# Loads and the large store of a graph layer moved from SyncE's queue to GpSimd's

## What is computed

```python
keep = (u >= 0.1).astype(x.dtype)
x_drop = x * keep / (1.0 - 0.1)
r = x + jnp.matmul(adj, x_drop)          # adj 8192 x 8192, x and u 8192 x 64, all fp32
m = jnp.mean(r, axis=-1, keepdims=True)
v = jnp.var(r, axis=-1, keepdims=True)
return (r - m) / jnp.sqrt(v + 1e-05)
```

## Time and profile before

| | us |
|---|---|
| median of 3 runs | 641.73 (641.69 to 641.83) |
| the profiled execution | 641.88 |
| its span | 640.1 |
| mean granted TensorE clock | 0.922 of full speed |
| PE busy | 502.8 (79% of the span) |
| DVE, ACT, POOL busy | 53.7, 17.7, 1.6 |
| HBM read, written | 272.63 MB, 2.10 MB: 429 GB/s over the span |

### The profile page before, as it was taken

One profiled execution on the slowest core, in us unless ns is written; L12 is line 12 of the kernel. 1 busy time (PEld: TensorE's weight loads), 2 busy tenths in 40 slices (PEclk: granted clock), 3 DMA queues, 4 the chain that ended last, 5 costly groups with the idle time before them and its releaser, 6 DMA issues.

```text
span 640.1 us, 5097 instructions
## 1 busy us (share of the span) xinstructions
PE 502.8 (79%) x2312; PEld 179.7 (28%) x2312; DVE 53.7 (8%) x102; ACT 17.7 (3%) x41; POOL 1.6 (0%) x14
## 2 busy tenths in 40 slices
PE   0097969688799578879878689867869868689997
PEld 0062213232233222223222223222323223133344
DVE  1930001010010100101000010100101001010101
ACT  0001000000000000000000000000000000000000
POOL 1000000000000000000000000000000000000000
PEclk9997979988799978889979899978999969799999
DMA  9999999999999999999999999999999999999998
GB/s 393 459 394 455 431 420 454 405 446 439 422 421 436 435 451 422 438 408 444 459 418 434 442 412 455 420 434 446 426 418 426 446 451 422 438 405 438 425 425 364
DMA packets 7207, 274.84 MB, mean 429 GB/s; under 512 B 800, under 2 KB 928, under 8 KB 1312
## 3 DMA queue, kind: packets, MB, share of 16 engines
q1 hardware_dynamic: 7056, 272.63, 98.8%
q10 hardware_dynamic: 144, 2.10, 0.8%
HBM read 272.63 MB, written 2.10 MB: 429 GB/s over the span
## 4 chain that ended last, share of the span: by engine, by line
DMA 62%; PE 33%; DVE 3%; another core or an unknown queue 1%; issue 0%; ACT 0%; SPq 0%; DVEq 0%; ACTq 0%
DMA ring<-adj 56%; PE acc L202 33%; DMA ring<-adj_last 5%; DMA xdrop<-u 2%; DVE node_sum L317 1%; DVE xdrop L321 1%; DVE xdrop L329 1%; PE folded L210 0%; DVE x_sb L321 0%; PE lifted L237 0%; SPq L126 0%; ACT squares L303 0%; PE lifted L263 0%; ACT std L308 0%
## 5 line engine op out<-in xcount | busy, mean ns | idle before, releaser
L202 PE MATMUL acc<-ring,xdrop 128*64 128x512 f32 (+1 forms) x2176 | 485.6, 606 | 103.1 <-DMA ring<-adj 101.7
L202 PEld LDWEIGHTS acc<-ring,xdrop 128*64 128x64 f32 x2176 | 162.8, 146 | 413.0 <-issue 280.2
L344 DVE SCALAR_TENSOR_TENSOR y<-folded,x_sb 128x256 f32<-128x256 f32 (+1 forms) x16 | 6.7, 416 | 552.3 <-PE folded L210 552.3
L237 PE MATMUL lifted<-x_sb,lift 128*128 128x64 f32 x4 | 1.1, 428 | 30.6 <-DVE x_sb L321 30.6
L210 PEld LDWEIGHTS folded<-fold,sums_T 128*128 128x128 f32 x128 | 15.5, 191 | 12.6 <-issue 12.6
L284 ACT COPY sums_T<-acc 128x512 f32<-128x512 f32 x15 | 8.8, 585 | 335.0 <-PE acc L202 335.0
L210 PE MATMUL folded<-fold,sums_T 128*128 128x64 f32 x128 | 17.7, 281 | 0.0
L277 ACT ACTIVATE std<-square_sum,eps 128x4 f32<-128x4 f32 (+1 forms) x16 | 4.8, 297 | 225.2 <-DVE square_sum L351 225.2
L237 PEld LDWEIGHTS lifted<-x_sb,lift 128*128 128x128 f32 x4 | 0.9, 322 | 30.5 <-issue 30.5
L348 DVE TENSOR_TENSOR squares<-y 128x256 f32<-128x256 f32 (+1 forms) x16 | 6.7, 417 | 0.5
L355 DVE TENSOR_TENSOR x_sb<-y,rstd 128x256 f32 (+1 forms) x16 | 6.7, 416 | 0.6
(11 more groups left out here) (23 smaller groups left out, 5.5 us busy)
## 6 DMA issues: line engine op xcount, KB each, us to landing
ring<-adj SPq DMA_DIRECT2D x13, 4096.0 KB, 31.3
ring<-adj SPq DMA_DIRECT2D x2, 2048.0 KB, 28.7
xdrop<-u ACTq DMA_DIRECT2D x1, 2048.0 KB, 12.5
x_sb<-x SPq DMA_DIRECT2D x1, 2048.0 KB, 12.3
out<-x_sb SPq DMA_DIRECT2D x1, 1984.0 KB, 12.7
ring<-adj_last SPq DMA_DIRECT2D x1, 1920.0 KB, 29.5
ring<-adj_last SPq DMA_DIRECT2D x1, 1792.0 KB, 33.4
ring<-adj_last SPq DMA_DIRECT2D x1, 1536.0 KB, 30.6
```

What stands on the lines that cost most here:

```text
L202: last = nc.tensor.matmul(acc[i][D * h:D * h + D, 0:cols], xdrop[:, k, :], piece[:, b, :], start=(k < 2), stop=(k >= NB - 2))
L344: nc.vector.scalar_tensor_tensor(out=y[:, 0:nj, :], in0=folded[:, 0:nj, :], scalar=1.0 / KEEP, in1=x_sb[:, bass.ds(block0, nj), :], op0=AL ...
```

## The change

The block of GpSimd now issues row 0, row 1, then makes its constants, and then issues all other loads of the matrix and the large store, with the same waits on `half_used` and `rows_ready`. SP keeps x, the last store and the final waits. The loop over t is gone: GpSimd's program is written out for rows 2 to 30. With no loop, rows 10 and 20 can be loaded as row 30 is, in one half and two quarters that signal `late_in`, and `late_free` with its memsets is gone. The large store has a semaphore of its own, `bulk_stored`. On PE the two products `lifted<-x_sb,lift` and their waits move from ahead of row 0 to behind it.

```diff
         @block.sync
         def _(sp):
             sp.dma_start(x_sb[:, :, :], x[:, :, :]).then_inc(x_in, 16)
-
+            sp.wait_ge(rows_ready, FINAL + 1)
+            sp.dma_start(out[:, NB - LAST_J:NB, :], x_sb[:, NB - LAST_J:NB, :]).then_inc(stored, 16)
+            sp.wait_ge(stored, 16)
+            sp.wait_ge(bulk_stored, 16)
+
+        @block.gpsimd
+        def _(pool):
             def load(r, w, first, count, arrived):
 
                 b = ((2 * w + 1) * HALF + first * QUARTER) % (RING * HALF)
-                sp.dma_start(ring[:, b:b + count * QUARTER, :],
+                pool.dma_start(ring[:, b:b + count * QUARTER, :],
                              adj[r - 1, :, first * QUARTER:(first + count) * QUARTER, :]).then_inc(arrived, 16)
...
-                sp.wait_ge(half_used, r * 2 + (half - (RING - 1)))
+                pool.wait_ge(half_used, r * 2 + (half - (RING - 1)))
...
-            sp.dma_start(narrow[:, first_narrow:first_narrow + LAST_PB, :],
+            pool.dma_start(narrow[:, first_narrow:first_narrow + LAST_PB, :],
                          adj_last[0, :, :, :]).then_inc(row_in[0], 16)
             whole(1, 1)
-            for w in range(2, WRAP):
-                free(w, 1)
-                whole(w, w)
-            wrapped(WRAP)
-            with sp.Fori(1, ROWS // RING - 1) as t:
...
-            for n in range(2):
-                nc.gpsimd.memset(late_free[:, n:n + 1], 0.0).then_inc(late_in[n], (ROWS // (2 * RING) - 1) * 16)
             nc.gpsimd.memset(eps[:, :], EPS).then_inc(eps_ready, 1)
...
+            for r in range(2, ROWS):
+                if r % RING == WRAP:
+                    wrapped(r)
+                    continue
+                free(r, 1)
+                if r % (2 * RING):
+                    whole(r, r % RING)
+                else:
+
+                    load(r, 0, 0, 2, row_in[0])
+                    for n in range(2):
+                        load(r, 0, 2 + n, 1, late_in[n])
+            for n, (k, size) in enumerate(parts):
+
+                free(ROWS, (k + size - 1) // (2 * HALF))
+                pool.dma_start(narrow[:, last_narrow + k:last_narrow + k + size, :],
+                             adj_last[1, :, k:k + size, :]).then_inc(part_in[n], 16)
+
+            pool.wait_ge(rows_ready, FINAL)
+            pool.dma_start(out[:, 0:NB - LAST_J, :], x_sb[:, 0:NB - LAST_J, :]).then_inc(bulk_stored, 16)
...
-            pe.wait_ge(lift_ready, 1)
-            pe.wait_ge(x_centred, 1)
-            for j in range(LAST_J):
-                nc.tensor.matmul(lifted[:, j, 0:D], lift[:, :], x_sb[:, NB - LAST_J + j, :], start=True, stop=False)
             pe.wait_ge(fold_ready, 1)
...
+            pe.wait_ge(lift_ready, 1)
+            pe.wait_ge(x_centred, 1)
+            for j in range(LAST_J):
+                nc.tensor.matmul(lifted[:, j, 0:D], lift[:, :], x_sb[:, NB - LAST_J + j, :], start=True, stop=False)
```

More of the change, by code:

```diff
@@ L60, in graph_layernorm @@
         node_sum = sb("node_sum", [P, 2, NB])
-        late_free = sb("late_free", [P, 2])
         fold = sb("fold", [P, D])
@@ L114, in graph_layernorm @@
         rows_ready = sem("rows_ready")
+        bulk_stored = sem("bulk_stored")
         stored = sem("stored")
```

## The result

The changed kernel takes 643.82 us (median of 7 runs, 643.76 to 644.12) against 641.83 us for the kernel before beside it (641.69 to 642.0): ratio 1.0032, 95% interval 1.0021 to 1.0043, 2.0 us slower. The forecast was 642.3, in a range of 637 to 652. The profiled execution took 643.76 us with a span of 642.0, against 640.1.

A forecast was written before the change was run, and what follows sets the result against it. The prediction took the DMA engines, 99.7% busy, as the bound. Span 640.1 + 0.1 (code) + 0.4 (pieces) + 0.1 (end) = 640.7, then + 1.78 outside the span - 0.15 to the median = 642.3 us, range 637 to 652.

The forecast's parts named there:

- The bound: Whole kernel: DMA queues fill 99.7% of the span, PE is busy 79%, so time is bytes over rate.
- equal rate: Loads in mid-kernel: GpSimd's queue moves bytes at the rate of SP's, 430 GB/s from 59 to 639 us.
- Rivals 2: Load transfers: a lower rate from more, smaller descriptors or lagging engines, 1 to 2.4%, 648 to 656 us; chance 0.17.
- rival 4: Long stretch of loads: GpSimd's queue takes up each DMA more cheaply, so a higher rate, 635 to 637.5 us; chance 0.22.
- The start: Opening loads: x and u share engines with row 0, DVE starts at 31.4 instead of 13.3 us, at no cost.
- Rival 1: Opening loads: x starved by GpSimd's queue, row 2 late, queue dry, up to 15 us lost, 644 to 657; chance 0.12.
- rival 3: Row 2's issue: GpSimd can't write descriptors while DVE works, 7.4 us lost, 650 us; chance 0.03.
- The issues: GpSimd's 51 DMA issues: nothing to 1.6 us extra each, hidden under a queue of 7.9 us; taken as 0.
- The pieces: Rows 10 and 20 in three DMAs each: 4 more DMAs at 0.1 us, +0.4 us, bounds 0 and 1.2.
- The end: Final stores: a slower completion of GpSimd's large store shows at once, 0 to +1.0 us, taken as +0.1.
- the likeliest case: Whole kernel: the forecast of 642.3 us itself, between 640.5 and 643.0; chance 0.42.
- The case of small costs at their upper bounds: Whole kernel: 1.2 us for more DMAs, 1 at the end, 0.5 for code, giving 644 us; chance 0.04.

## Why the prediction was right or wrong

- **The bound, and equal rate**: right. 430 GB/s before and after in the long stretch. Rivals 2 and 4 fall: the queue's owner changes neither the rate nor the price of a DMA. The Trainium skill's table in "DMA: Bandwidth & Descriptors" (Bandwidth, Measured) ends at 425 GB/s for the software path; the trace has 430 through it over 580 us (428 over the span), and the measurement decides. That engines 7 or 15 lag under it shows in no total here; single engines are not shown.
- **The start**: right in mechanism and price. T, the time from which DVE has x and u, was 27.9 us, not 31.4, since x and u had the engines to themselves until GpSimd's first packets at about 4 us. Row 2 was issued at 41.69 instead of at 45.1, earlier than the 44 to 46 that were named as the sign, because x came earlier; the 13.7 us from DVE's start to it were right. The run with x behind two rows has T = 52.1. By the prediction that costs a microsecond for each behind 34.6, 17.5 us, and 16.9 were measured. It is one point, so it bears out the two numbers together and neither alone. Rival 1 fell, though its price was real.
- **DVE and descriptors** (rival 3): row 2's DMA was issued at 41.69, with DVE busy from 27.94 to 52.2, and took 0.55 us where others take 0.53. Its only wait was for PE. With the queue full this shows nothing of how soon its descriptors were there. The run with x behind two rows does: the queue was empty, DVE was busy from 52.10 past 76 us, and the first packets came 1.2 us after the issue at 66.34. Rival 3 falls for DVE instructions like these (1024 elements in 1.22 us).
- **The issues**: 0, as taken. GpSimd needs 0.53 us for one, SP 0.33, both hidden.
- **The pieces**: 0.1 us each taken, 0.077 to 0.09 measured. Four of them are 0.3 us; what is seen ahead of the last product is 0.2, which is within the noise. Fifty are 3.9 us, so the number of DMAs is at most a part of the gap between 430 and 440 GB/s (14.5 us) on which rival 4 was built.
- **The end**: this step failed. It asked whether the large store would complete later and gave that 0 to 1.0 us, taking 0.1. The store completed as before (12.3 us, 12.7 before). What was missing is an instruction that is in no line of the diff: the drain that the end of the block puts on every engine. It was in the trace before, 0.38 us long at 2.4 us, and the prediction priced only instructions that the diff names. It is a term of 51 x 0.043 = 2.2 us behind the landing, of which 1.7 to 1.8 reach the end, since before the end lay 0.4 us behind the last store. With it the sum would have been 642.3 - 0.1 + 1.8 = 644.0, against 643.82.
- **What held the prediction together without being priced**: that the large store stays behind the parts. The text named it as a reason for no cost; two runs show it was worth 4.6 and 5.9 us at the last product. By the Trainium skill ("DMA: Bandwidth & Descriptors", Issuing engines are not separate DMA queues) all queues run on the same 16 engines and interleave. The runs agree, 1.16 MB against 0.16 in one stretch of 3 us (73 packets against 40), and show the price: sharing the engines delays the transfer that is wanted first.
- The time fell outside the likeliest case's own range (640.5 to 643.0). The case of small costs at their upper bounds, 644 at a chance of 0.04, has the number, by a mechanism that it did not contain. That the measured time lies in the range of 637 to 652 owes nothing to insight into the end: the range was that wide for the rate and the start, whose rivals fell.

No version here beats the kernel before.

## What to carry to other kernels

Look at what the program's end adds to each engine, and ask which engine will be last there: here GpSimd's drain cost 0.043 us for every DMA it had issued, behind the last landing, so GpSimd is the wrong issuer for many DMAs if one of its own ends the program. Keep transfers whose order matters in one queue, the wanted ones first; a second queue shares the engines at once and gives a late, large transfer its turn ahead of an urgent one. With the DMA engines full, the questions are only bytes, the number of DMAs (0.08 us each) and whether the queue is ever dry, and a dry moment is paid about one for one (16.4 us dry, 16.9 lost).

## What the runs showed of the hardware that was not expected

- GpSimd's drain is the longer the more DMAs GpSimd issued: 4.23 us for 51 and 0.14 us for one when all have landed; 2.2 us are left for 51 if it began 12 us before the last landing, and 2.07 for 50 if it began 37 us before. The head start beyond 12 us bought nothing.
- One handover from SP's queue to GpSimd's in mid-stream put the last product 17.2 us later, by starving the row in use of its turns.
- Each DMA cost the saturated engines 0.077 us, on SP's queue and on GpSimd's.
- The first packets of a load that GpSimd issued to idle engines showed 1.2 us after the issue, with DVE busy beside it.
